# The first slot of a pipelined attention stage: keys turned ahead of batch 1's rows and tables, row statistics ahead of the context's scale, B's rows squared a slot later

## The reference

```
x = layernorm(x + autocorrelation_attention(x))      # rfft, |f|^2, irfft, top 7 lags, softmax, gather
x = layernorm(x + cross_attention(ctx, ctx, x))      # per batch: sim = ctx @ x^T / 16, softmax over keys, sim @ ctx
x = layernorm(x + x @ W_base^T + moe_lora(x))        # 8 experts of rank 8, A and B small, top 2 of 8
```

## Time and profile before

| | us |
|---|---|
| median of 3 runs (lowest, highest) | 1966.44 (1965.95, 1971.0) |
| the profiled execution, its own time | 1964.43 |
| its span in the trace | 1962.6 |
| TensorE busy | 1779.3 (91%) |
| VectorE busy | 1361.5 (69%) |
| ScalarE busy | 791.6 (40%) |
| DMA, mean of the core's 16 engines | 241 GB/s |

### The profile page before, as it was taken

How to read it: one execution, slowest core, us unless ns; L and a number is a source line. 1 busy time by engine, 2 the same in 40 slices (tenths; PEclk the granted TensorE clock), 3 DMA queues, 4 the chain that set the end, 5 groups by cost and what they waited for, 6 DMA issues and landing times. The chain is left out here.

```text
span 1962.6 us, 27015 instructions
## 1 busy us (share of the span) xinstructions
PE 1779.3 (91%) x10194; PEld 953.8 (49%) x10210; DVE 1361.5 (69%) x2605; ACT 791.6 (40%) x939; POOL 200.1 (10%) x358
## 2 busy tenths in 40 slices
PE   3989999999853959999999999998899999999997
PEld 2656665767531425445544445443344444444443
DVE  3878888888859866777666777799654655565463
ACT  5888888788745211222222212133231222213111
POOL 1223232323200000000000000000010010010000
PEclk9999999999975989999999999999999999999998
DMA  8899999999758499999999999945999879988882
GB/s 279 196 278 269 287 249 288 269 282 257 223 199 239 113 240 254 269 255 236 247 256 266 250 227 227 231 164 161 294 259 253 274 221 259 266 249 252 248 242 108
DMA packets 565563, 472.70 MB, mean 241 GB/s; under 512 B 498416, under 2 KB 502512, under 8 KB 544624
## 3 DMA queue, kind: packets, MB, share of 16 engines
q1 hardware_dynamic: 565424, 470.87, 87.8%
HBM read 237.51 MB, written 109.58 MB: 177 GB/s over the span
## 5 line engine op out<-in xcount | busy, mean ns | idle before, releaser
L1558 PE MATMUL bank_f<-w_hi_f,a_cols_f 128*128 128x512 f16 x3584 | 1090.4, 381 | 78.0 <-DVE w_lo_f L1292 36.4
L1558 PE MATMUL bank_f<-w_lo_f,a_cols_f 128*128 128x512 f16 x1792 | 683.6, 381 | 0.0
L1558 PEld LDWEIGHTS bank_f<-w_hi_f,a_cols_f 128*128 128x128 f16 x3584 | 352.2, 98 | 507.4 <-DMA a_cols_f<-rows_f 41.7
L1148 ACT ACTIVATE rows_f<-xn_f 128x1024 f16<-128x1024 f32 x78 | 82.4, 1057 | 500.1 <-DMA xn_f<-x_scratch 337.8
L1558 PEld LDWEIGHTS bank_f<-w_lo_f,a_cols_f 128*128 128x128 f16 x1792 | 176.0, 98 | 204.0 <-issue 3.2
L1323 DVE SCALAR_TENSOR_TENSOR y_f<-bank_f,w_iscale_f,y_f 128x512 f32<-128x512 f32 x192 | 134.5, 742 | 169.3 <-PE bank_f L1558 169.2
L649 PE MATMUL ps_s_fast<-k_both_fast,q_hi_fast 128*128 128x256 f16 x1024 | 170.8, 275 | 7.4 <-DMA k_both_fast<-v_lo_fast 6.4
L1284 DVE TENSOR_TENSOR rows_f<-xn_f,rows_f 128x1024 f16<-128x1024 f32 x78 | 94.3, 1209 | 97.6 <-ACT rows_f L1148 97.6
L1323 DVE SCALAR_TENSOR_TENSOR y_f<-bank_f,w_iscale,y_f 128x512 f32<-128x512 f32 x192 | 134.7, 743 | 34.8 <-PE bank_f L1558 31.6
L1284 DVE TENSOR_TENSOR rows_f<-sums_f,rows_f 128x1024 f16<-128x1024 f32 x63 | 76.8, 1219 | 114.8 <-ACT rows_f L1148 114.6
L1148 ACT ACTIVATE rows_f<-sums_f 128x1024 f16<-128x1024 f32 x63 | 66.3, 1052 | 195.9 <-DMA a_cols_f<-rows_f 193.3
(11 more groups left out here) (210 smaller groups left out, 2300.8 us busy)
## 6 DMA issues: line engine op xcount, KB each, us to landing
xbuf_fast<-x SPq DMA_DIRECT2D x32, 1024.0 KB, 7.8
x_scratch<-x2buf_fast SPq DMA_DIRECT2D x32, 1024.0 KB, 5.7
y_f<-x_scratch SPq DMA_DIRECT2D x32, 1024.0 KB, 7.8
xn_f<-x_scratch SPq DMA_DIRECT2D x62, 512.0 KB, 4.9
kept_scratch<-a_cols_f SPq DMA_DIRECT2D x45, 512.0 KB, 3.4
xn<-x_scratch SPq DMA_DIRECT2D x45, 512.0 KB, 6.8
a_cols_f<-kept_scratch SPq DMA_DIRECT2D x45, 512.0 KB, 8.7
cbuf<-ctx_in SPq DMA_DIRECT2D x16, 1024.0 KB, 5.9
```

The costliest lines, as they stand in the source:

```text
L1148: nc.scalar.activation(rows[g % 2][:, 0], source(i), ACT.Copy).then_inc(a_hi, 1)
L1558: ins = nc.tensor.matmul(bank[i][:], a_cols[:, i, part + kk, :], ww[:, W_SLOT[i], kk, :], start=(kk == 0 and part == 0 and ww is w_hi), st ...
```

## The change

Four edits, all in slot -2 or at the start of slot -1.

1. SyncE in slot -2: the high part's two transposes are issued before any row of batch 1; the first row tile of batch 1 comes between the high and the low part; the second row tile, B's rows and the two tables come behind the last transpose and the last context tile.
2. VectorE in slot -2: `x_stats(0)` runs ahead of `context_scale`, and `x_stats(1)` ahead of both `value_low`.
3. ScalarE in slot -2: `normalise1(0)` runs between `value_high(0)` and `value_high(1)`.
4. ScalarE: B's rows are squared in slot -1, ahead of the four squares of batch 1's context, no longer in slot -2.

```diff
+                def load_x_rows(n, parity, r):
+                    after(sp, ctx_added, CG * (n - 2) + NBANK * (r + 1))
+                    sp.dma_start(xbuf[parity][:, r], src[bass.ds(n * C + r * P, P), :]).then_inc(x_loaded[parity][r], 16)
...
                         load_x(0, 0)
-                        load_x(1, 1)
+                        for r in range(R):
+                            transpose_keys(0, 0, 0, r)
+                        load_x_rows(1, 1, 0)
+                        for r in range(R):
+                            transpose_keys(0, 0, 1, r)
+                            load_context(1, r)
+                        load_x_rows(1, 1, 1)
                         load_weights(0)
                         sp.dma_start(fwd[:], consts["fwd_dram"]).then_inc(tables_loaded, 16)
                         sp.dma_start(inv[:], consts["inv_dram"]).then_inc(tables_loaded, 16)
+                        return
...
-                    def square_weights(i):
+                    def square_weights(n, i):
...
                     if n == -1:
+                        square_weights(-2, 0)
+                        square_weights(-2, 1)
                         for i in range(PIECES):
                             square_context(i)
...
                     value_high(0)
+                    if n == -2:
+                        normalise1(0)
+                        value_high(1)
+                        normalise1(1)
+                        return
                     value_high(1)
                     normalise1(0)
                     softmax_exp(0)
-                    square_weights(0)
-                    square_weights(1)
+                    square_weights(n, 0)
+                    square_weights(n, 1)
...
-                    if n != -1:
+                    if n > -1:
                         context_scale()
...
                     x_stats(0)
-                    if n == -1:
+                    if n < 0:
                         context_scale()
+                    if n == -2:
+                        x_stats(1)
+                        value_low(0)
+                        value_low(1)
+                        return
                     value_low(0)
```

More of the change, by code:

```diff
@@ L249, in load_x @@
                         for r in range(R):
-                            after(sp, ctx_added, CG * (n - 2) + NBANK * (r + 1))
-                            sp.dma_start(xbuf[parity][:, r], src[bass.ds(n * C + r * P, P), :]).then_inc(x_loaded[parity][r], 16)
+                            load_x_rows(n, parity, r)
                 def slot(n, half, parity):
```

## The result

| | before | after |
|---|---|---|
| median, runs side by side (us) | 1967.33 (9 runs, 1965.14 to 1971.54) | 1977.79 (9 runs, 1972.58 to 1981.28) |
| ratio, 95% interval | | 1.0046 (1.0036 to 1.0056) |
| profiled execution, own time and span | 1964.43, 1962.6 | 1975.69, 1973.9 |

The change makes the kernel slower by 0.46%, about 9.0 us (7.1 to 11.0); 7.2 us were forecast. The ratio is not the quotient of the two medians, which would be 1.0053 or 10.5 us; both say the same within the interval.

What follows compares the result with a forecast made beforehand. The lead-in, where first logits and context squares meet at about 49 us, was taken to set every following slot. B's late rows delay it 7.2 us: 1966.44 + 7.2 = 1973.6 us, range 1966.0 to 1978.0.

Steps and rivals of the forecast that it cites:

- The step that decides: ScalarE, slot -1: waits for B's rows before the context's squares, so batch 1's v_hi starts at 56.8, 7.2 us later.
- First v_hi at 17.1, second over at 23.0, last transpose at 39.4: Lead-in times on ScalarE and SyncE's queue; keys turned only 1.5 us earlier than 40.9.
- The pairs of 6.05 us: SyncE's queue: a load with a low-half transpose behind it takes 6.05 us to issue, from 25.2 and from 31.3.
- GpSimd beside statistics: GpSimd's four steps for the first norm's constants run beside VectorE's statistics without hold-up, done by about 17.7.
- upper-end term of 0.9: If GpSimd's steps were held up, they end at about 19.9 and everything behind moves 0.9 us later.
- B's rows: SyncE's queue: B's rows land at 48.1, 2.8 us after x's second row tile at 45.3.
- The time: Whole kernel: 7.2 us later, median 1973.6 us; the forecast's chance 0.60.
- the cover: TensorE: 2.3 us more for slow second logits stay hidden before the row maximum; if not, 0 to 0.5 us.
- What lies beside: Earlier second norm and first logits gain nothing; slow second logits and the later weight tile are covered.
- Absorbed: Rival: later slots, DMA engines busy 0.99 of the time, swallow the slip; about 1966.4 to 1968, chance 0.13.
- Short slip: Rival: transfers go near the low bound, 2.2 to 5.8 us later, 1968.6 to 1972.2; chance 0.18.

Runs made afterwards that it cites:

- e1: The changed kernel with B's load moved right behind batch 0's rows, ahead of the transposes; ratio 0.9990 to the kernel before.
- e3: The changed kernel with VectorE's and ScalarE's old orders in slot -2, queue order and B's squares as changed; ratio 1.0029 to the kernel before.
- e2: The kernel before with only B's squares moved to slot -1, ahead of the context's squares; ratio 0.9999.
- e8: The kernel before with only the new VectorE and ScalarE orders in slot -2; ratio 0.9999.
- e5: e4 with batch 1's first row tile of x loaded behind the last context tile; ratio 0.9977 to the kernel before.
- e6: The changed kernel with B's rows laid out as 128 partitions of 1024; ratio 1.0024 to the kernel before.
- e4: e3 with B's load right behind batch 0's rows; ratio 0.9981 to the kernel before.
- e7: All four transposes ahead of batch 1's loads, B loaded early and squared in slot -2, VectorE and ScalarE as before; ratio 0.9963 to the kernel before.
- e10: e9 with both tables loaded straight behind B's rows, ahead of the first transposes; ratio 0.9968 to the kernel before.
- e9: e7 with batch 1's context scale ahead of the statistics in slot -1; ratio 0.9986 to the kernel before.

## Why the prediction was right

*The step that decides* held in every part. ScalarE's wait for B's rows, with their load behind everything, is what costs: e1 moves the load alone and lands 9.3 us of v_hi earlier, slightly below the kernel before, and e3 keeps the late load and loses 5.8 us without the compute edits. Those add 2.5 us, by the same wait. The place of the squares alone (e2) and the compute orders alone (e8) cost nothing. The late load with the squares at their old place was not run; there ScalarE would meet the same wait in slot -2, ahead of the second norm and the q halves, so I would not expect it to be harmless.

*First v_hi at 17.1, second over at 23.0, last transpose at 39.4.* Measured 17.01, 22.9 and 39.5. The pairs of 6.05 us came as 6.9 (24.28 to 31.15) and 6.25 (31.20 to 37.45), and started 0.9 earlier. The two errors nearly cancel, so that 39.4 came out so well is in part luck; e5 shows the hold-up behind a load by itself.

*GpSimd beside statistics.* Its four steps ended at 17.65, before the v_hi was over; the second set began with a 2.17 us step beside the first v_lo. So the upper-end term of 0.9 did not occur, and the trace agrees with the rule of the Trainium skill ("SBUF — State Buffer", Who interferes with whom) on both sides: one SBUF input, no hold-up; two, a hold-up as long as the v_lo.

*B's rows.* Forecast at 48.1, landed at 49.2. This is the term that was mis-sized, by 1.1 us: the tile ahead and B's rows took 5.8 from the context tile's landing, where I had 2.4 + 2.8 and had started 0.5 too early. I had put the 2.8 on B's rows alone; e6 shows that B's form also delays the tile ahead of it (47.3 instead of 45.7).

*The time.* 1977.79 is 4.2 us above the forecast 1973.6. Of this 1.1 are B's rows, and 0.9 the kernel before, whose median was 1967.33 in these runs and not 1966.44. Another 0.7 lie between the gap in v_hi (8.3 us) and the ratio (9.0), and 1.4 between the ratio and the medians (10.5); neither can be told from noise, as all three lie in the interval of 7.1 to 11.0. That the median still fell into the range owes something to luck: the high end held 0.9 for GpSimd and 0.5 for the cover, and neither occurred.

*What lies beside.* The second logits began at the slow pace after the 9.45 us stand. They took 6.6 us (58.02 to 64.60), where 7.6 was feared and 5.3 is the full pace, and this stayed covered, as forecast: p_lo is later by exactly what v_hi is. The stretches of the changed kernel also show the granted clock:

```profile
38.00:40.00 2.00, 0.43 (x3) 0.50 1.21 190
40.00:42.00 2.00, 2.00 (x11) 0.50 0.91 373
44.00:46.00 2.00, 2.00 (x21) 1.00 1.15 348
58.00:60.00 2.00, 1.98 (x10) 0.50 0.03 8
62.00:64.00 2.00, 2.00 (x21) 1.00 1.36 176
```

(columns: stretch, length, TensorE busy, clock, DMA share, GB/s.) At 0.50, which is 1.2 GHz, some 10 matmuls fit into 2 us, at 1.00 some 21. In the kernel before the same slow pace from 40.9 to 45 carries a clock of 1.00, and so it does in e3, e6 and e8, so there the column doesn't tell and the count of matmuls does.

*Absorbed* was wrong for a slip: e3, e6 and the change carry 5.8, 5.1 and 8.3 us of lead-in to 5.7, 4.7 and 9.0 at the end, all within their intervals. For a gain there is something in it. The times of e4, e5, e7 and e10 give 3.7, 4.5, 7.3 and 6.3 us of 5.5, 7.0, 8.6 and 7.7. For e5 (interval 2.6 to 6.7) and e9 (0.6 to 4.9), whose intervals leave their shifts out, the traces show 3.5 and 3.2 us lost within the one slot that follows. A late lead-in shifts the transfers with it; in e5, e7 and e9 the early one meets a queue that is still busy with the loads ahead (see e7). How much is lost in the slots after that is not settled: all gaps are taken against one profiled execution of the kernel before, and from batch 5 to the last they drift by 0.5 to 3.2 us in the same direction for late and early kernels alike, e9 excepted.

*Short slip* did not occur: it needed transposes whose issue isn't held behind a load, and both low halves were held 5.5 to 5.6 us.

What stays open: why e9's time lies above e7's, how much of an early lead-in the later slots give back, and why a load ahead holds up a transpose's issue at all.

## What to carry to other kernels

When a load is moved to the back of a queue, look for its consumer in program order on its engine, not at when its result is needed: an instruction that nobody waits for still holds up all that is queued behind it. In a pipeline's lead-in, write down the two or three chains that meet before the first full slot and ask which ends last; a wait that shows up on the engine with the most work (here TensorE's for the keys) need not be it. In this kernel the best order (e7) put the transposes back to back, not a load ahead of each.

## What the runs showed of the hardware that was not expected

- A DMA transpose issued straight behind a fresh 1 MB load keeps the issuing queue 5.3 to 5.8 us; with no fresh load ahead 1.8 to 2.3 us (e5: 5.56 and 2.29 in one kernel; e8 has the 5.33, e5 the 5.75).
- A 0.5 MB load into 64 partitions of 8 KB rows cost 2.3 us more than the same bytes over 128 partitions of 4 KB rows, and 1.6 of that fell on the load ahead of it (e6).
- The granted clock in a profile can read 1.00 while matmuls come at half pace (the kernel before, 40.9 to 45 us: a 128x256 every 0.21 us; e3, e6 and e8 too); in the changed kernel, e1 and e2 the same pace reads 0.50.
